# A fused audio tower on one core: 32 of 65 dense chunk steps move from the picks stages into attention, 12 more into gradient and preparation

## The reference, cut to what matters

```python
h = token_mixer(x)                      # tanh layers, then a 15-tap convolution of stride 2: 375 tokens of 64
h = h + retention(layernorm(h))         # rotary q and k, decayed scores, no softmax
h = h + memory_attention(layernorm(h))  # below
h = h + learned_memory(layernorm(h))    # gradient of a 2-layer net over ALL images, one AdamW step, then retrieval
h = h + experts(layernorm(h))           # 8 experts, the best one for each token

def memory_attention(x, Wq_pk, pk_keys, Wq, keys_table, values_table, Wo):
    q = (x @ Wq).reshape(b, n, 8, 64) * 64 ** -0.5
    # product keys: for each token and head the 16 best of 64 x 64 pairs, and their softmax weights
    scores, idx = top_k(einsum('pbnhd,pkhd->pbnhk', (x @ Wq_pk)..., pk_keys), 16)
    final_scores, pk_idx = top_k(all 256 sums of scores[0] and scores[1], 16)
    w = softmax(final_scores)
    k = einsum('bnhk,bnhkd->bnhd', w, keys_table[ind])      # 4096 rows for each head
    v = einsum('bnhk,bnhkd->bnhd', w, values_table[ind])
    sim = causal(einsum('bihd,bjhd->bhij', q, k))
    return concat(softmax(sim) @ v) @ Wo
```

## Time and profile before

| | |
|---|---|
| median of 3 runs | 9592.07 us |
| lowest and highest | 9579.78, 9598.28 us |
| the profiled execution's own time | 9655.03 us |
| its span in the trace | 9653.2 us |
| granted clock, mean (1 is 2.4 GHz) | 0.625 |

### The profile page before, as it was taken

How to read it: one execution, slowest core, us unless ns; L and a number is a source line. 1 busy time by engine, 2 the same in 40 slices (tenths; PEclk the granted TensorE clock), 3 DMA queues, 4 the chain that set the end, 5 groups by cost and what they waited for, 6 DMA issues and landing times.

```text
span 9653.2 us, 88445 instructions
## 1 busy us (share of the span) xinstructions
PE 6021.4 (62%) x24336; PEld 4056.4 (42%) x24336; DVE 3291.4 (34%) x14095; ACT 2054.4 (21%) x4455; POOL 4290.6 (44%) x4574
## 2 busy tenths in 40 slices
PE   1466666566666656665665756566666655656587
PEld 1344444344444434444443444434344433434453
DVE  4234250433425043251514324152332504234026
ACT  0122221212222121221212222121222212122132
POOL 2453536445362644536355353635535364453500
PEclk7565655656566565656657565665657566565667
DMA  1111101111010111101011110101101011110100
GB/s 38 52 38 27 39 21 47 32 32 41 24 43 20 46 33 30 39 24 45 23 41 38 27 39 22 46 26 38 37 26 40 23 45 31 34 39 23 42 11 13
DMA packets 166415, 321.93 MB, mean 33 GB/s; under 512 B 81980, under 2 KB 90772, under 8 KB 165710
## 3 DMA queue, kind: packets, MB, share of 16 engines
q0 software_dynamic: 144384, 295.20, 11.7%
q1 hardware_dynamic: 21166, 20.00, 0.8%
q10 hardware_dynamic: 288, 0.07, 0.0%
HBM read 310.37 MB, written 4.61 MB: 33 GB/s over the span
## 4 chain that ended last, share of the span: by engine, by line
another core or an unknown queue 34%; PE 29%; issue 18%; DVE 15%; ACT 4%; DVEq 0%; ACTq 0%; DMA 0%; SPq 0%
PE gath L601 6%; PE accu L467 5%; PE dense L457 4%; ACT past L841 2%; PE dense L452 2%; PE dense L458 1%; PE work L624 1%; DVE mx L1293 1%; PE sims L570 1%; DVE picks L1229 1%; DVE idxf L1233 1%; PE work L585 1%; DVE ranks L1243 1%; DVE picks L1239 1%
## 5 line engine op out<-in xcount | busy, mean ns | idle before, releaser
L417 POOL DMA_INDIRECT store<-in,idx_now x4512 | 4274.3, 947 | 4483.6 <-PE gath L601 2623.1
L601 PEld LDWEIGHTS gath<-wbd,store 128*128 128x128 f32 (+1 forms) x9024 | 1562.1, 260 | 720.0 <-issue 681.1
L601 PE MATMUL gath<-wbd,store 128*128 128x8 f32 (+1 forms) x9024 | 1511.6, 300 | 529.4 <-issue 440.6
L457 PE MATMUL dense<-parts_f,hot 128*128 128x375 bf16 x3072 | 880.2, 408 | 813.9 <-issue 687.8
L841 ACT ACTIVATE past<-dense,edge 128x375 bf16<-128x375 f32 x1024 | 588.8, 575 | 3017.6 <-remote 2309.9
L452 PE MATMUL dense<-ranksT,hot 128*128 128x375 bf16 x1008 | 398.0, 395 | 1322.5 <-ACT past L841 1109.8
L467 PE MATMUL accu<-dense_w,store 128*128 128x375 f32 x2048 | 1094.8, 625 | 12.9 <-issue 10.9
L457 PEld LDWEIGHTS dense<-parts_f,hot 128*128 128x128 bf16 x3072 | 307.6, 112 | 1246.5 <-issue 1172.3
L452 PEld LDWEIGHTS dense<-ranksT,hot 128*128 128x128 bf16 x1008 | 152.2, 151 | 1552.5 <-issue 1482.7
L849 ACT ACTIVATE dense_w<-dense 128x375 f32<-128x375 f32 x1024 | 493.8, 482 | 1130.7 <-remote 656.9
L467 PEld LDWEIGHTS accu<-dense_w,store 128*128 128x128 f32 x2048 | 488.9, 252 | 136.0 <-issue 100.6
(11 more groups left out here) (276 smaller groups left out, 7041.3 us busy)
## 6 DMA issues: line engine op xcount, KB each, us to landing
store<-in,idx_now POOLq DMA_INDIRECT x4512
x_in<-in SPq DMA_DIRECT2D x16, 187.5 KB
store<-in SPq DMA_DIRECT2D x1, 2048.0 KB, 8.4
queries_kept<-n3T SPq DMA_DIRECT2D x16, 93.8 KB
h_saved<-h SPq DMA_DIRECT2D x16, 93.8 KB
store<-queries_kept SPq DMA_DIRECT2D x16, 93.8 KB, 2.4
store<-h_saved SPq DMA_DIRECT2D x16, 93.8 KB
out<-store SPq DMA_DIRECT2D x16, 93.8 KB
```

Of the source, the lines that this page charges most:

```text
L417: nc.gpsimd.indirect_dma_start(rows[0:slots, r * PER + i, :], None, kv_table, bass.IndirectOffsetOnAxis(ap=idx_now[0:slots, at:at + 1], ax ...
L457: mm(dense[:, 1, 0:S], hot[:, c, :], parts[:, k, h, :], start=(k == 0), stop=False)
L601: last = mm(gath[:, 0, at:at + 8], rows[0:slots, r * PER + i, :], wbd[0:slots, t * GATHERS + n, :], start=True, stop=True)
```

## The change

All 65 steps remain, and all 36 groups stand where they stood. An image's steps were 9 in gradient, 12 in preparation and 44 in the two picks stages. Now 14 are in gradient, 19 in preparation and none in the picks stages: the first dense head and the first of the second. The other 32 steps run inside attention: two before head 0, and five in each of heads 0 to 5, two ahead of the mix and three between the two halves of the transposes. The last image has the same 32 inside, and FILL_LAST holds groups alone.

For that the memory is parted. Queries and the rotary products go to a buffer of their own (`two_q`), odd heads' probabilities to `prob_odd`, the mix to the bank `gath`, and the third tile's picks indices from `dense` to `places_s`; `halves` takes up `nT`, `n2T_now`, `dz` and the rotary table. Both halves of the transposes go through bank 1 of `work`, one after the other, so ScalarE copies the first half (`half_done`) before TensorE makes the second. The outputs of the last head (`last_outputs`) are made later, before its scores, when the second dense head is done.

```diff
-FILL_GRADIENT = ((0, 2), (3, 2), (2, 1), (2, 1), (2, 2))
-FILL_PREPARE = ((1, 1), (1, 1), (1, 1), (1, 1), (2, 1), (1, 1), (2, 1), (1, 1), (2, 1))
-FILL_PICKS = (((12, 4), (10, 3)),) * 2
-FILL_LAST = (44, 14)
+FILL_GRADIENT = ((0, 2), (4, 2), (3, 1), (3, 1), (4, 2))
+FILL_PREPARE = ((2, 1), (2, 1), (2, 1), (2, 1), (3, 1), (2, 1), (2, 1), (2, 1), (2, 1))
+FILL_PICKS = (((0, 4), (0, 3)),) * 2
+FILL_LAST = (0, 14)
+FIRST_HEAD, STEPS_A, STEPS_B = 2, (2, 2, 2, 2, 2, 2, 0, 0), (3, 3, 3, 3, 3, 3, 0, 0)
...
-                    if c == 0 and h == 0:
-                        pe.wait_ge(s["h2_done"], b + 1)
...
+                if g == 0 and t == 0:
+                    pe.wait_ge(s["h2_done"], b + 1)
...
             def attention(b, turned_picks, following):
...
-                pe.wait_ge(s["acc_done"], b * HD + HD)
+                pe.wait_ge(s["acc_done"], b * HD + HD - 1)
...
-                        last = mm(accu[0:P, 0, i * D:(i + 1) * D], pT[:, c // 3, at:at + P], vo[:, j, h * D:(h + 1) * D],
+                        last = mm(gath[0:P, 0, i * D:(i + 1) * D], pT[:, c // 3, at:at + P], vo[:, j, h * D:(h + 1) * D],
...
+                dense_steps(b, FIRST_HEAD)
                 for h in range(H):
+                    if h + 1 == H - 1:
+                        pe.wait_ge(s["acc_done"], b * HD + HD)
                     if h + 1 < H:
                         scores(h + 1)
+                    if h + 1 == H - 1:
+                        last_outputs()
                     if h + 2 < H:
                         queries(h + 2)
+                    dense_steps(b, STEPS_A[h])
                     if h >= 1:
                         mix(h - 1)
                     pe.wait_ge(s["s_norm"], b * H + h + 1)
                     for c, (i, j, at) in enumerate(PAIRS):
-                        dst = work[0:P, 1, at:at + P] if c < 3 else dense[0:P, 0, at:at + P]
-                        last = tr(dst, prob[h % 2][:, c // 3, at:at + P], ident[0:P, 0:P])
+                        if c == 3:
+                            dense_steps(b, STEPS_B[h])
+                            pe.wait_ge(s["half_done"], b * H + h + 1)
+                        last = tr(work[0:P, 1, at:at + P], prob[h % 2][:, c // 3, at:at + P], ident[0:P, 0:P])
+                        if c == 2:
+                            last.then_inc(s["half_mm"], 1)
                     last.then_inc(s["pT_mm"], 1)
...
                 scale_q(0)
                 scale_q(1)
+                dense_steps(b, FIRST_HEAD)
                 exponentials(0)
                 for h in range(H):
...
                     if h + 2 < H:
                         scale_q(h + 2)
+                    dense_steps(b, STEPS_A[h])
                     if h + 1 < H:
                         exponentials(h + 1)
                     if h == H - 2 and soften_next is not None:
                         soften(*soften_next)
+                    act.wait_ge(s["half_mm"], b * H + h + 1)
+                    nc.scalar.copy(pT[:, 0, :], work[0:P, 1, 0:S]).then_inc(s["half_done"], 1)
+                    dense_steps(b, STEPS_B[h])
                     act.wait_ge(s["pT_mm"], b * H + h + 1)
-                    nc.scalar.copy(pT[:, 0, :], work[0:P, 1, 0:S])
-                    nc.scalar.copy(pT[:, 1, :], dense[0:P, 0, 0:S]).then_inc(s["pT_done"], 1)
+                    nc.scalar.copy(pT[:, 1, :], work[0:P, 1, 0:S]).then_inc(s["pT_done"], 1)
```

More of the change, by code:

```diff
@@ L59 @@
 FILL_TURN = ((0, 3), (0, 2))
-FILL_GRADIENT = ((0, 2), (3, 2), (2, 1), (2, 1), (2, 2))
-FILL_PREPARE = ((1, 1), (1, 1), (1, 1), (1, 1), (2, 1), (1, 1), (2, 1), (1, 1), (2, 1))
-FILL_PICKS = (((12, 4), (10, 3)),) * 2
-FILL_LAST = (44, 14)
+FILL_GRADIENT = ((0, 2), (4, 2), (3, 1), (3, 1), (4, 2))
+FILL_PREPARE = ((2, 1), (2, 1), (2, 1), (2, 1), (3, 1), (2, 1), (2, 1), (2, 1), (2, 1))
+FILL_PICKS = (((0, 4), (0, 3)),) * 2
+FILL_LAST = (0, 14)
 FILLS = FILL_TURN + FILL_GRADIENT + FILL_PREPARE + sum(FILL_PICKS, ())
-assert sum(f[0] for f in FILLS) == STEPS + 1 and sum(f[1] for f in FILLS) == NT * GROUPS
+FIRST_HEAD, STEPS_A, STEPS_B = 2, (2, 2, 2, 2, 2, 2, 0, 0), (3, 3, 3, 3, 3, 3, 0, 0)
+INSIDE = FIRST_HEAD + sum(STEPS_A) + sum(STEPS_B)
+assert sum(f[0] for f in FILLS) == STEPS + 1 - INSIDE and STEPS + 1 - INSIDE > STEPS - CHUNKS and sum(f[1] for f in FILLS) == NT * GROUPS
 HID, E = 256, 8
@@ L243, in tower @@
         dense = bank("dense", 2)
-        place_banks = (sims[0:P, 0], sims[0:P, 0], dense[0:P, 1])
+        place_banks = (sims[0:P, 0], sims[0:P, 0], places_s[:])
         names = """loaded_first loaded fold_mm fold_done prep tapd x_in tok_mm tok_act tok_sq conv h0_done ln_stats
@@ L540, in prepare @@
                 for c in range(2):
-                    mm(work[0:D, c, 0:S], wrope_s[:, c], nT[:], start=True, stop=True)
-                    last = mm(sims[0:D, c, 0:S], wrope_s[:, 2 + c], nT[:], start=True, stop=True)
+                    mm(work[0:D, c, 0:S], wrope_s[:, c], nT, start=True, stop=True)
+                    last = mm(sims[0:D, c, 0:S], wrope_s[:, 2 + c], nT, start=True, stop=True)
                 last.then_inc(s["qk_mm"], 1)
@@ L621, in attention @@
                     if j >= 1:
-                        pe.wait_ge(s["vo_done"], b * NT + j)
-                    for h in range(H):
+                        pe.wait_ge(s["vo_done"], b * (NT + 1) + j)
+                    for h in range(H - 1):
                         last = mm(work[0:P, 0, h * D:(h + 1) * D], kvT[D:128, h, tile(j)], wo_s[D:128, h, :],
@@ L626, in attention, with last_outputs @@
                     last.then_inc(s["vo_mm"], 1)
-                pe.wait_ge(s["vo_done"], b * NT + NT)
+                pe.wait_ge(s["vo_done"], b * (NT + 1) + NT)
+                def last_outputs():
+                    for j in range(NT):
+                        last = mm(work[0:P, 0, j * D:(j + 1) * D], kvT[D:128, H - 1, tile(j)], wo_s[D:128, H - 1, :],
+                                  start=True, stop=True)
+                    last.then_inc(s["vo_mm"], 1)
                 def queries(h):
-                    mm(work[0:D, 0, 0:S], wq_s[:, h], n2T_now[:], start=True, stop=True).then_inc(s["q_mm"], 1)
+                    mm(work[0:D, 0, 0:S], wq_s[:, h], n2T_now, start=True, stop=True).then_inc(s["q_mm"], 1)
                 def scores(h):
@@ L827, in keep @@
                 nc.scalar.copy(h1_now[:], h1[:])
-                nc.scalar.copy(n2T_now[:], n2T[:]).then_inc(s["kept"], 1)
+                nc.scalar.copy(n2T_now, n2T[:]).then_inc(s["kept"], 1)
             step = [0]
@@ L889, in prepare @@
                 act.wait_ge(s["nT_mm"], b * 2 + 1)
-                nc.scalar.copy(nT[:], work[0:D, 1, 0:S]).then_inc(s["nT_done"], 1)
+                nc.scalar.copy(nT, work[0:D, 1, 0:S]).then_inc(s["nT_done"], 1)
                 between()
@@ L949, in attention @@
                 for j in range(NT):
-                    act.wait_ge(s["vo_mm"], b * NT + j + 1)
-                    nc.scalar.copy(vo[:, j, :], work[0:P, 0, :]).then_inc(s["vo_done"], 1)
+                    act.wait_ge(s["vo_mm"], b * (NT + 1) + j + 1)
+                    nc.scalar.copy(vo[:, j, 0:(H - 1) * D], work[0:P, 0, 0:(H - 1) * D]).then_inc(s["vo_done"], 1)
                 def scale_q(h):
@@ L963, in attention @@
                 scale_q(1)
+                dense_steps(b, FIRST_HEAD)
                 exponentials(0)
                 for h in range(H):
+                    if h + 1 == H - 1:
+                        act.wait_ge(s["vo_mm"], b * (NT + 1) + NT + 1)
+                        nc.scalar.copy(vo[:, :, (H - 1) * D:], work[0:P, 0, 0:NT * D].rearrange("p (j d) -> p j d", d=D)).then_inc(s["vo_done"], 1)
                     if h + 2 < H:
                         scale_q(h + 2)
+                    dense_steps(b, STEPS_A[h])
                     if h + 1 < H:
@@ L1122, in prepare @@
                 dve.wait_ge(s["qk_mm"], b + 1)
-                v.tensor_tensor(qk[:], work[0:D, :, 0:S], rope_t[:, 0], ALU.mult).then_inc(s["rope_a"], 1)
+                v.tensor_tensor(qk, work[0:D, :, 0:S], rope_t[:, 0], ALU.mult).then_inc(s["rope_a"], 1)
                 v.tensor_tensor(qk_b, sims[0:D, :, 0:S], rope_t[:, 1], ALU.mult).then_inc(s["rope_b"], 1)
```

30 lines of the change are left out of this document (18 added, 12 removed).

## The result

The changed kernel takes 10044.95 us (median of 4, 10012.61 to 10060.18), the kernel before 9585.92 us beside it: a ratio of 1.0483, with an interval of 1.0441 to 1.0525. Forecast were 10525 us.

A forecast was written before the change was run, and what follows sets the result against it. The prediction took the kernel as bound outside attention by gathers that slow the engines' short operations; 28 + 25 + 9 = 62 us an image, 15 times, plus the ends, gave 10525 us, range 9400 to 11300 (the forecast's own 10250 to 10900).

The forecast's parts named there:

- What bounds the kernel: Outside attention, gathers slow the engines; VectorE and gathers bind the first picks stage, and the second ends with TensorE's 25 us.
- 1.10 us of VectorE's progress lost for each gather: Picks stages: each gather beside VectorE's short operations costs it 1.10 us, on top of 54 us without gathers.
- 54 + 72 x 1.10 = 133: Second picks stage: all 72 gathers come before the long operations, so it takes 133 us, +1 us.
- 54 + 38 x 1.10 = 96: First picks stage: all 38 gathers come before the long operations, so it takes 96 us, +8 us.
- picks term: Both picks stages, which lose 44 steps: +8 us in the first and +1 in the second, an image.
- third run stays late: Second picks stage: the last gathers still go under the long operations; picks -25 us an image, about 10020 us; chance 0.21.
- Attention +28: Attention with 32 steps: six heads +22 us, two steps ahead +5.5, two heads without steps +1; bounds +14 and +82.
- so I take 0.85: Attention: TensorE's clock assumed 0.85 with five steps in a head, so 13.1 us a head.
- rival of a cold attention: Attention's clock stays at 1.2 GHz: +82 us there, 121 an image in all, about 11400 us; chance 0.11.
- Gradient and preparation +25: Gradient and preparation: 12 more steps, mostly on the path, at 2.1 us each, +25 us an image; bounds 17 and 33.
- faster rival: Picks stages: the steps' instructions take VectorE's issue slots, so gathers get cheaper without them; about 9150 us; chance 0.22.
- The ends: Outside the loop's 15 images: +10 us in the first image's gradient, -3 us in the last image.

The follow-up runs named there:

- first_held: The changed kernel with 20 steps inside attention, 12 in the second picks stage, and TensorE waiting for VectorE's short operations before the first picks stage's last four groups: 9440.68 us.
- twelve_back: The changed kernel with gradient and preparation back at 9 and 12 steps, the other 12 in the second picks stage: 9543.85 us, 0.9951 of before.
- more_in_gradient: The changed kernel with 18 and 27 steps in gradient and preparation, 20 inside attention, and a TensorE wait in the second picks stage: 9827.53 us, 1.0201 of before.
- prepared_again: The kernel of first_held with 9 steps in gradient and 24 in preparation, where it has 14 and 19: 9386.6 us, 0.9788 of before.
- emptied_again: The kernel of first_held with 3 steps in gradient and 30 in preparation, where it has 14 and 19: 9544.76 us, 0.9962 of before.

## Why the prediction was wrong, step by step

- **What bounds the kernel.** Right where the crawl is met, and shown: a hold that adds a wait makes the kernel faster, and without the crawl the two picks stages shrink to 57 and 66 us. What failed is its step "1.10 us of VectorE's progress lost for each gather", one price for all. "54 + 72 x 1.10 = 133" came near: in the 13 images with all 72 before the long operations, VectorE ended 131 us into the stage. But the 7.4 us behind it, `turn_picks`, the cast and the copy, were put at about 2, so the stage is 136.6 on the mean. "54 + 38 x 1.10 = 96" failed: 36 to 39 gathers did come before the long operations, but VectorE's part ended after 77 to 87 us, 82 on the mean, or (82 - 54) / 38 = 0.74 us for each. In first_held the last 14 are held back and it ends at 76, so these 14 cost 0.4 each and the first 24 (76 - 54) / 24 = 0.92: a new run's first gathers cost little, as the rows above show. The picks term was +9 and measured +3.
- **The rival "third run stays late".** It came in one second picks stage of 15 in one execution and in three of 15 in another.
- **Attention +28.** The step "so I take 0.85" failed: a clock of 0.85 was put on every head with steps, where it is 1.00 in all six, and 0.53 only in the products ahead of them. The mean of 0.87 over the stage looks like the number assumed, but it holds those. Of the term's parts, the heads came as 11.6 and not 22, the two steps ahead of head 0 as 4.5 and not 5.5, the two heads without steps as nothing and not 1: 16 in all, two above the lower bound. The rival of a cold attention is refuted by the same rows. The Trainium skill's rule on transposes (TensorE: Matmul & The Clock Gate, Part 4: PE-mode transpose) takes the transposes out of what warms the clock; it says nothing of the steps among them, so "by that rule alone attention stays cold" asked too much of it. No run contradicts the rule itself. With five, three or even two full-array steps in a head attention isn't cold: 0.87, 0.79 and 0.74.
- **Gradient and preparation +25.** This step failed most: "I take 2.1" for each of twelve steps. They cost 5.9 us together against the kernel before, 9.1 against twelve_back. I had counted each step as one on the path and at a mean clock of about 0.6. Means of 14 images show both parts of the error. TensorE's busy time in the two stages grew by 18.0 us (162.0 to 180.0), 1.5 a step, near the 1.43 of the earlier trace rows, while the stages' mean clocks rose from 0.56 and 0.63 to 0.61 and 0.70. And its time without work fell by 12.1 us (95.6 to 83.5): two thirds of what the steps took lay in waits that were there anyway. In more_in_gradient, prepared_again and emptied_again further steps cost between nothing and 3 us each in one of these stages, and what decides it stays open.
- **The faster rival** (the steps' own instructions make a gather dear) is refuted: with TensorE idle 79 us of the second stage, 72 gathers cost VectorE (131 - 54) / 72 = 1.07 us each.
- **The ends.** +10 was forecast for the first image's gradient, and the loop's first product comes 6.6 us later (433.3 to 439.9). -3 was forecast for the last image, and 22.2 came off between the last two adds (463.9 to 441.7), although one gradient of the loop, longer by some 6, lies in that stretch. Attention grew by 24.5 us there and not 35: 92.4 us from its first scores to its end (9569.47 to 9661.9) against 67.9 before (9236.97 to 9304.9). The steps outside gave back some 52 us, where -43, -10 and +15 made 38; which of the three was off isn't shown.

Together: 15 x 62 + 7 = 937 was forecast, and 31.4 + 14 x 24.8 - 22.2 = 357 came. All three terms of an image were too large, so the sign was right for the reasons given and the size was not.

## What to carry to other kernels

When short operations crawl beside another engine's indirect gathers, the count of gathers matters less than how long they run unbroken and what they run beside: look where in a run the crawl begins, and put the rest of the run under long operations or idle stretches, with a wait if need be. Work taken off an engine that seemed late may have been what kept such a run in its place; ask what will start earlier. A full-array step among small products pays for a part of itself through the clock, so price it by the clock it brings. A filler's price in one stage (nothing to 3 us here) can't be carried to the next dozen: measure it again.

## What was not expected of the hardware

- One and the same program took some 9590 us on two chips and 6751 on a third. The gathers take as long on both (0.94 and 0.97 us), but in the first case VectorE's short operations wait 1.31 us and TensorE's small products 2.64 us for nothing that the profile shows.
- That crawl doesn't depend on a gather's size: 128 rows or 16, 35 GB/s or 4.
- It isn't there from a run's start. VectorE starts 60 operations beside a run's first six gathers and 15 beside the next six, and once the run has ended 3 to 4 us pass before it is back at its pace. Where GpSimd paused for 3.79 us before its third run, the stage was 26 us shorter.
